# A routed mixture-of-experts layer: first token tile dense during routing, 21 steps over seven tiles, second bias on VectorE, step weights by dynamic DMA

## What is computed

```python
def reference(X, ...):                       # X [1, 1024, 256]
    Q, K, V = split(X @ W_in.T + b_in)       # rotary on the first half of Q and K
    A = sum_over_tokens(K / |K| * V)
    x = layernorm(X + (A * Q) @ W_out.T + b_out + X)
    probs = softmax(x @ gate_w)              # [1024, 8]
    score, idx = top_k(probs, 2)             # normalised to sum 1
    combine = onehot(idx) * score * alpha    # [1024, 8], two entries a row
    h = gelu(x @ fc1_w[e] + fc1_b[e])        # per expert, 256 to 256
    y = h @ fc2_w[e] + fc2_b[e]
    out = layernorm(x + sum_e combine[:, e] * y)
```

## Time and profile before

| | us |
|---|---|
| median of three runs | 142.26 |
| lowest, highest | 141.44, 142.46 |
| span of the profiled execution, first to last instruction | 139.7 |
| TensorE matmul busy in it | 117.2 (84%) |
| weight load on TensorE | 99.4 (71%) |
| VectorE, ScalarE, GpSimd busy | 71.7, 63.6, 50.9 |
| mean granted clock of TensorE | 0.936 |

### The profile page before, as it was taken

The page is one execution under the profiler, slowest core; times in us unless marked ns, Lnnn a source line. Parts: engine busy times, 40 slices in busy tenths (PEclk is TensorE's granted clock), DMA queues, the critical chain, the costliest instruction groups (busy, mean ns, idle before and its releaser), DMA issues.

```text
span 139.7 us, 2236 instructions
## 1 busy us (share of the span) xinstructions
PE 117.2 (84%) x696; PEld 99.4 (71%) x696; DVE 71.7 (51%) x209; ACT 63.6 (45%) x156; POOL 50.9 (36%) x77
## 2 busy tenths in 40 slices
PE   7799998997989838587899999999999999606920
PEld 7678887796879728475788888888888887603800
DVE  0459858796776897769433332523121222023480
ACT  3535968434653000437448475665745426000270
POOL 3008998177000001832454335574534434300000
PEclk9999999999997896899999999999999999995595
DMA  3899999951222000221122121231221221278235
GB/s 110 250 320 426 399 353 348 348 165 46 109 75 80 0 0 0 77 75 42 38 82 68 42 75 38 70 113 49 75 75 46 69 69 48 75 229 284 88 125 175
DMA packets 11209, 18.01 MB, mean 129 GB/s; under 512 B 1269, under 2 KB 7614, under 8 KB 10942
## 3 DMA queue, kind: packets, MB, share of 16 engines
q1 hardware_dynamic: 9662, 13.68, 28.8%
q0 software_dynamic: 1536, 4.20, 9.4%
HBM read 13.68 MB, written 4.19 MB: 128 GB/s over the span
## 4 chain that ended last, share of the span: by engine, by line
PE 48%; DVE 18%; POOL 11%; DMA 10%; SPq 4%; issue 4%; ACT 2%; DVEq 1%; POOLq 0%
PE ps L1148 16%; PE ps L1136 14%; PE ps L1146 5%; DMA gT_hi<-pair_rows 4%; DMA bo<-in_b_out 4%; POOL x L371 3%; POOL x L372 2%; PE ps L1119 2%; DVE lane_hot L811 2%; DMA pair_rows<-kv,scatter_i 2%; SPq L306 2%; PE ps L1040 2%; PE ps L964 2%; POOL kv L375 2%; PE ps L1029 1%
## 5 line engine op out<-in xcount | busy, mean ns | idle before, releaser
L1136 PEld LDWEIGHTS ps<-early,w_now 128*128 128x128 f32 x184 | 23.9, 191 | 3.4 <-issue 2.4
L1136 PE MATMUL ps<-early,w_now 128*128 (+1 forms) x184 | 24.5, 276 | 1.8 <-DVE early L874 1.8
L1148 PE MATMUL ps<-wres,g 128*128 x92 | 26.0, 405 | 0.0
L915 DVE SCALAR_TENSOR_TENSOR kv<-ps,w_step,kv 128x256 f32 x23 | 11.1, 483 | 28.4 <-PE ps L1148 23.7
L549 ACT ACTIVATE g<-ps,b_step 128x128 f32<-128x128 f32 x46 | 14.4, 364 | 23.6 <-PE ps L1136 23.5
L413 POOL DMA_INDIRECT pair_rows<-kv,scatter_i x16 | 15.6, 973 | 15.2 <-DVE kv L915 13.6
L972 PE MATMUL ps<-ones 128*128 128x128 f32 x100 | 17.7, 351 | 2.6 <-DVE pick_b L869 1.6
L406 POOL DMA_INDIRECT gT_hi<-x_rows,gather_i x8 | 8.4, 1048 | 28.6 <-DVE gather_i L824 20.9
L565 ACT COPY w_now<-wres 128x512 f32 x23 | 14.0, 616 | 10.4 <-issue 10.4
L972 PEld LDWEIGHTS ps<-ones 128*128 128x128 f32 x100 | 16.7, 260 | 2.8 <-issue 1.8
L1148 PEld LDWEIGHTS ps<-wres,g 128*128 128x128 f32 x92 | 15.6, 189 | 4.1
(11 more groups left out here) (181 smaller groups left out, 209.9 us busy)
## 6 DMA issues: line engine op xcount, KB each, us to landing
wres<-in_expert_w SPq DMA_DIRECT2D x8, 512.0 KB, 9.1
early<-in_x_t SPq DMA_DIRECT2D x4, 256.0 KB, 5.8
acc<-in_x_tok SPq DMA_DIRECT2D x1, 1024.0 KB, 8.6
rT<-in_rope_t SPq DMA_DIRECT2D x1, 1024.0 KB, 9.9
x_rows<-x SPq DMA_DIRECT2D x4, 256.0 KB, 2.6
gT_hi<-pair_rows SPq DMA_DIRECT2D x4, 256.0 KB, 3.7
gT_lo<-pair_rows SPq DMA_DIRECT2D x4, 256.0 KB, 6.4
out<-z SPq DMA_DIRECT2D x4, 256.0 KB, 2.2
```

Of the source, the lines that this page charges most:

```text
L915: v.scalar_tensor_tensor(out=part, in0=two(Y_BANK, s), scalar=w_step[:, s:s + 1], in1=part, op0=ALU.mult, op1=ALU.add).then_inc(y_ok, 1)
L1136: last = nc.tensor.matmul(two(H_BANK, s)[:, tile(m)], w1_now[:, s % W1_SLOTS, k, tile(m)], x[:, tile(k)], start=k == 0, stop=k == KD - 1)
L1148: last = nc.tensor.matmul(dst, g[:, s % 2, k, :], weights(KD + k, s), start=False, stop=k == KD - 1)
```

## The change

- The routed part takes tiles 1 to 7 only: 1792 choices, 14 tiles of slots, 21 steps. All tables, lists and buffers of the routing shrink accordingly.
- Tile 0 is computed dense: each of the 8 experts on its 128 tokens (`dense_fc1`, `dense_fc2`), scaled by that token's entry of `combine` (`comb0`, zero for experts not chosen) on ScalarE, added up on GpSimd (`dense_add`) onto `x1`. Its second bias is one product of `comb0T` with the 8 bias rows. Seven experts stand in TensorE's order between gates and steps, in the place of the warming products there, the eighth behind the last step. GpSimd does four of the adds before its first gather, four between the fourth and fifth gather, and one behind the last scatter.
- The alpha and tanh parts of the weights move: the weights wt are worked out before VectorE waits for the positions, alpha after the one-hot lists.
- The second bias of a step is added by VectorE, as `y_plus`, from all bias rows held on every partition (`b2_all`, a 1 MB load ahead of tables and expert weights); TensorE waits for this first instruction (`y_read`) before it writes the bank again. The bias product, `pick_b2` and the conversion of `b2` on GpSimd go.
- A step's first weights come from memory into one of four slots by an SP DMA whose source is offset by a register (`experts`, loaded on SP), 256 KB each; the copies on ScalarE and its register loads go. The slots lie in what was `rT`.
- The end: no pair for tile 0; odd tiles are added by VectorE, tiles 2, 4, 6 by GpSimd, none by TensorE, and its 12 warming products go.

```diff
-STEPS = 23
+STEPS = 21
-W1_SLOTS = 3
+W1_SLOTS = 4
...
+            sp.dma_start(b2_all[:], fc2_b.rearrange("e d -> (e d)").partition_broadcast(P)).then_inc(l_b2_all, 16)
             sp.dma_start(tab[:], tables).then_inc(l_tab, 16)
...
+            sp.wait_ge(e_no_ok, 1)
+            experts = loaded(SP, e_no, E - 1, "counts of E - 1 comparisons")
+            for s in range(STEPS):
+                if s >= W1_SLOTS:
+                    sp.wait_ge(fc1_mm, s - W1_SLOTS + 1)
+                sp.dma_start(w1_now[:, s % W1_SLOTS, :, :],
+                             expert_w[bass.ds(experts[s], 1), :, 0:KD, :].rearrange("e p k d -> p (e k) d"))\
+                  .then_inc(w1_in[s % W1_SLOTS], 16)
             sp.wait_ge(scattered, 16 * TS)
-            for t in range(T):
+            for t in range(FIRST_ROUTED, T):
...
+            def dense_add(n):
+                pool.wait_ge(d_y_ok, n + 1)
...
+            pool.wait_ge(x1_ok, 1)
+            for n in range(4):
+                dense_add(n)
...
             pool.wait_ge(idx_ok, 1)
+            for i in range(GATHERED_FIRST):
+                gather(i)
+            for n in range(4, DENSE_AHEAD + 1):
+                dense_add(n)
+            for i in range(GATHERED_FIRST, TS):
+                pool.wait_ge(xs_ok, i - GATHERED_FIRST + 2)
                 gather(i)
             pool.wait_ge(scatter_ok, 1)
             for i in range(TS):
                 scatter(i)
+            for n in range(DENSE_AHEAD + 1, E + 1):
+                dense_add(n)
+            for t in POOL_SUMS:
+                pool.wait_ge(l_pair[t], 16)
+                g_.tensor_tensor(acc[:, t, :], pair(t, 0), pair(t, 1), ALU.add).then_inc(pool_sum_ok, 1)
...
             x1_across(4)
+            a.copy(x0T[:], x1T[:, 0, :, :]).then_inc(x0T_ok, 1)
...
             a.activation(th[:], gap[:], ACT.Tanh, scale=0.5).then_inc(th_ok, 1)
+            def dense_gelu(e):
+                act.wait_ge(d_fc1_mm, e + 1)
...
+            def dense_out(n):
+                act.wait_ge(d_fc2_mm, n + 1)
+                if n >= 2:
+                    act.wait_ge(d_sum_ok, n - 1)
...
+            dense_gelu(0)
+            dense_gelu(1)
+            act.wait_ge(comb0_ok, 1)
+            dense_out(0)
+            act.wait_ge(comb0T_mm, 1)
+            a.copy(comb0T[:], ps[0:E, COMB_BANK, 0:P]).then_inc(comb0T_ok, 1)
+            for e in range(2, DENSE_AHEAD):
+                dense_gelu(e)
+                dense_out(e - 1)
+            dense_out(DENSE_AHEAD - 1)
+            dense_out(DENSE_AHEAD)
...
+                v.tensor_tensor(y_plus[:, s % 2, :], two(Y_BANK, s), b2_all[:, bass.ds(at_expert, D)],
+                                ALU.add).then_inc(y_read, 1)
+                dve.wait_ge(y_read, s + 1)
...
-                v.scalar_tensor_tensor(out=part, in0=two(Y_BANK, s), scalar=w_step[:, s:s + 1], in1=part,
+                v.scalar_tensor_tensor(out=part, in0=y_plus[:, s % 2, :], scalar=w_step[:, s:s + 1], in1=part,
...
-            stay_warm(WARM_ROUTE[0], WARM_BANK)
...
+            dense_fc1(0)
+            dense_fc1(1)
+            dense_fc2(0)
+            places()
+            dense_fc1(2)
+            pe.wait_ge(comb0_ok, 1)
+            nc.tensor.transpose(ps[0:E, COMB_BANK, 0:P], comb0[:], ident[:]).then_inc(comb0T_mm, 1)
+            dense_fc2(1)
+            dense_fc1(3)
+            dense_fc2(2)
+            inverted(0)
+            inverted(1)
+            dense_fc1(4)
+            inverted(2)
+            inverted(3).then_inc(inv_mm, 1)
+            dense_fc2(3)
+            for e in range(5, DENSE_AHEAD):
+                dense_fc1(e)
+                dense_fc2(e - 1)
+            dense_fc2(DENSE_AHEAD - 1)
+            dense_fc2(DENSE_AHEAD)
             pe.wait_ge(w_off_ok, 1)
             e_off = loaded(PE, w_off, (E - 1) * D, "counts of E - 1 comparisons")
...
-                pe.wait_ge(w1_now_ok, s + 1)
+                pe.wait_ge(w1_in[s % W1_SLOTS], 16 * (s // W1_SLOTS + 1))
...
-                nc.tensor.matmul(dst, pick_b2[:, s:s + 1].to_broadcast([BIAS_ROWS, P]), b2_parts[:], start=True, stop=False)
...
-            stay_warm(WARM_TAIL, WARM_BANK)
...
+            pe.wait_ge(g_ok, 2 * STEPS)
+            pe.wait_ge(y_read, STEPS)
+            for e in range(DENSE_AHEAD, E):
+                dense_fc1(e)
+                dense_fc2(e + 1)
```

More of the change, by code:

```diff
@@ L541, in _ @@
             a.activation(th[:], gap[:], ACT.Tanh, scale=0.5).then_inc(th_ok, 1)
+            def dense_gelu(e):
+                act.wait_ge(d_fc1_mm, e + 1)
+                if e >= 2:
+                    act.wait_ge(d_fc2_mm, e - 1 if e <= DENSE_AHEAD + 1 else e)
+                for m in range(KD):
+                    a.activation(g0[:, e % 2, m, :], two(H_BANK, e)[:, tile(m)], ACT.Gelu,
+                                 bias=b1[:, e, m:m + 1]).then_inc(d_g_ok, 1)
+            def dense_out(n):
+                act.wait_ge(d_fc2_mm, n + 1)
+                if n >= 2:
+                    act.wait_ge(d_sum_ok, n - 1)
+                e = dense_expert(n)
+                a.activation(y0[:, n % 2, :], two(Y_BANK, n), ACT.Copy,
+                             scale=1.0 if n == DENSE_AHEAD else comb0[:, e:e + 1]).then_inc(d_y_ok, 1)
             def gelu(s):
@@ L906, in _ @@
             dve.wait_ge(w_step_ok, 1)
+            dve.wait_ge(l_b2_all, 16)
             def y_add(s):
                 dve.wait_ge(fc2_mm, s + 1)
+                at_expert = nc.s_assert_within(s * D - offs[s], 0, (E - 1) * D,
+                                               skip_runtime_bounds_check_because="a step's expert is the step less its tile")
+                v.tensor_tensor(y_plus[:, s % 2, :], two(Y_BANK, s), b2_all[:, bass.ds(at_expert, D)],
+                                ALU.add).then_inc(y_read, 1)
+                dve.wait_ge(y_read, s + 1)
                 dve.wait_ge(acc0_ok, min(s + 1, TS))
@@ L1104, in _, with dense_fc1, dense_fc2 @@
-            stay_warm(WARM_ROUTE[2], WARM_BANK)
+            def dense_fc1(e):
+                if e >= 2:
+                    pe.wait_ge(d_g_ok, 2 * e - 2)
+                for m in range(KD):
+                    for k in range(KD):
+                        last = nc.tensor.matmul(two(H_BANK, e)[:, tile(m)], wres[:, k, e, tile(m)], x0T[:, k, :],
+                                                start=k == 0, stop=k == KD - 1)
+                last.then_inc(d_fc1_mm, 1)
+            def dense_fc2(n):
+                if n >= 2:
+                    pe.wait_ge(d_y_ok, n - 1)
+                if n == DENSE_AHEAD:
+                    pe.wait_ge(comb0T_ok, 1)
+                    nc.tensor.matmul(two(Y_BANK, n), comb0T[:], b2[:], start=True, stop=True).then_inc(d_fc2_mm, 1)
+                    return
+                e = dense_expert(n)
+                pe.wait_ge(d_g_ok, 2 * e + 2)
+                for k in range(KD):
+                    last = nc.tensor.matmul(two(Y_BANK, n), g0[:, e % 2, k, :], wres[:, KD + k, e, :],
+                                            start=k == 0, stop=k == KD - 1)
+                last.then_inc(d_fc2_mm, 1)
@@ new lines, in _, with places @@
+            flat = chosen[:].rearrange("p t e -> p (t e)")
+            def places():
+                pe.wait_ge(earlier_ok, 1)
+                pe.wait_ge(all_ones_ok, 2)
+                pe.wait_ge(z_ok, T)
+                pe.wait_ge(chosen_ok, 1)
+                nc.tensor.matmul(ps[:, POS_BANK, 0:(RT + 1) * E], earlier[:], flat, start=True, stop=False)
+                for back in range(1, RT + 1):
+                    last = nc.tensor.matmul(ps[:, POS_BANK, back * E:(RT + 1) * E], all_ones[:], flat[:, 0:(RT + 1 - back) * E],
+                                            start=False, stop=back == RT)
+                last.then_inc(pos_mm, 1)
@@ new lines, in inverted @@
+            def inverted(group):
+                pe.wait_ge(tile_id_ok, group + 1)
+                pe.wait_ge(hot_ok, group + 1)
+                for i in range(*HOT_GROUPS[group]):
+                    last = nc.tensor.matmul(ps[:, INV_BANK, INV_AT:INV_AT + 3 * TS], lane_hot[:, i, :],
+                                            tile_id[:, i, :, :].rearrange("p a j -> p (a j)"),
+                                            start=i == 0, stop=i == 2 * RT - 1)
+                return last
+            pe.wait_ge(l_exp, 16 * E)
@@ L1228 @@
         everywhere(np.arange(SLOT_TILES) * P),
[L1229 to L1230 removed]
+        everywhere(np.tile(tiles[T - ROUTED:], 2)),
+        everywhere(np.repeat(np.arange(2), ROUTED)),
         everywhere(np.arange(E)[None, :] < np.arange(E)[:, None]),
         lanes[:, None],
[L1233 removed]
         everywhere(np.arange(STEPS)),
```

269 lines of the change are left out of this document (126 added, 143 removed).

## The result

The median of four runs is 131.48 us (129.00 to 132.97), that of the kernel before beside them 142.36. The same kernel run again with the experiments gave 129.74 (ratio 0.913, 0.903 to 0.923). The forecast was 133.7, with 130.8 as the lower end of its wider range, and 0.914 of 142.26 is 130.0: right in direction, too small in size. The profiled execution is that of 129.00; its span is 12.8 us shorter than in the earlier trace rows.

The account below looks back on a forecast made before the run. TensorE's unbroken chain was taken to bound the loop, VectorE the stretch before it. Loop -10.0, routing +3.1, last step 0, end -1.7 sum to -8.6: 142.26 to 133.7 us; range 131.5 to 136, wider 130.8 to 138.

Parts of the forecast that it names:

- the price of the bias product: Loop: removing it saves 0.28 us per step, bounds 0.12 and 0.31; steps 1.98 us, or 2.20 with a transpose.
- a slow first step: Loop start: 0.3 us added to the loop for VectorE's register load.
- Rival (a): Loop: the bias product's pause stays with fc2, 0.11 saved per step for 0.28; +3.2, 136.9 us; chance 0.14.
- Routing: Stretch before the loop: dense experts of tile 0 make fc1(2) start 3.1 us later; bounds +1.5 and +5.
- The positions: Routing stretch: position products queue behind fc2(0), so VectorE reads them at 49.0 instead of 47.06, +1.9 us.
- its register load: Routing stretch: TensorE's load of 21 values, 2.1 us, uncovered after dense work; first transpose 59.94 to 63.5, +3.6.
- rival (b): Routing stretch: GpSimd (POOL) becomes the queue that counts, gather 4 some 3.5 us late; +3, 136.7 us; chance 0.10.
- The end: After the loop: last sum +0.5, bias products -0.6, net 0; final reload and statistics -1.7 us.
- The dense tile's last expert: After the last y sum: expert 7 of tile 0, 4.6 us, done before the first pair lands.
- the 1 MB bias load: Start: 2.9 us more loading, all in at 34 before weights are read at 43; costs nothing, otherwise up to +2.9.
- rival (c): Loop: weight loads run the four slots dry, step 2.65 us; +9.8, 143.5 us; chance 0.08 shared with all-dense-work-at-lower-clock.
- Rival (d): Routing stretch: dense experts run at lower clock; +10, 143.7 us; partly 0.05, whole within 0.08 shared with slow weight loads.

Follow-up runs that it names:

- a_evict0_late: The kernel after with VectorE's first eviction moved behind the plan's first three instructions; 129.05 us, ratio 0.910 to the kernel before.
- a_extra_load: The kernel after with one more 256 KB load at the head of the final reload, nothing computed from it; 133.66 us (one run).
- b_tail_sums: The kernel before with only the pair sums moved off TensorE to GpSimd and VectorE, eight pairs as before; 141.57 us, ratio 0.995.
- b_bias_dve: The kernel before with only the second bias moved from a TensorE product to VectorE, with its 1 MB load; 133.01 us, ratio 0.934.
- a_w1_act: The kernel after with the steps' first weights copied by ScalarE again instead of loaded by SP's DMA; 131.26 us, ratio 0.924 to the kernel before.
- a_again: The kernel after, unchanged, run again beside the experiments; 129.74 us, ratio 0.913 to the kernel before.
- b_all_again: The kernel before with every part of the change except the dense tile, second run; 136.49 us, ratio 0.956.
- a_late_behind2: The kernel after with the late first eviction and two experts of tile 0 behind the loop instead of one; 132.50 us, ratio 0.937.

## Why the prediction fell short

**The failed step is the price of the bias product.** I bounded it by 0.12 and 0.31 us and took 0.28; it was 0.51. The upper end wasn't one. It came from "fc2 to fc1 and fc1 to the bias product cost no such pause in the chain (both take 0.97 to 0.98 from start to start)". That equality showed only that both had the same pause. The eight products of an fc1 take 0.89 and the four of an fc2 0.865 when nothing with fewer rows stands next to them. The trace of before held the hint: the bias product of the earlier trace rows (99.82) and its weight load began at the same moment, and so did fc2 (100.13) and its:

```profile
99.82 0.18 PEld L1146 LDWEIGHTS ps<-b_parts,pick_b 40*128 40x128 f32 x1
100.13 0.73 PEld L1148 LDWEIGHTS ps<-wres,g 128*128 128x128 f32 x4
```

18 steps by 1.98 - 1.755 = 0.225 are 4.05 us; 0.9 went back in a slow first step and the wait at 80.51 beyond the 0.3 allowed, and 3.1 are left, the whole difference in the loop's line. Rival (a) had the sign of this doubt wrong: fc2 kept no pause, it lost one.

**Routing: right in sum (+3.3 for +3.1, where 1 us is the line's own spread), with two errors that cancel.** The positions came 1.5 us later from the mark, not 1.9. TensorE stood for its register load behind the last dense product, as forecast, but that product ended at 61.4, not 62.0, and the transpose followed 0.8 us later: most of the 1.8 us load ran beside the products. So it came at 62.20 and not 63.5, from the mark 2.8 us later and not 3.6. From there I took half a us off and half a us came on: L938 and L940 took 0.63 and 1.02 us, 0.34 and 0.59 before for slightly more columns. That is rival (b)'s mechanism at another place. They ran beside GpSimd's four adds (62.68, 3.46 us); in a_evict0_late, ahead of the adds, they took 0.33 and 0.53. There L959, beside the adds now, took 0.87 instead of 0.47. DMA traffic is not the reason: the core moved 215 GB/s beside the slow one and 242 beside the fast one. The Trainium skill (GPSIMD Engine Reference, Specifications) names contention of GpSimd with VectorE instructions that have two SBUF inputs. The trace agrees in that these instructions read two SBUF operands, while evictions from PSUM stayed at 0.42; but not each instruction with two was slowed (beside the adds of a_evict0_late L952 and L956 took 0.31 and 0.47, as elsewhere). It did not reach the loop as (b) feared: the y sums kept 0.42 and 0.48, and gather 4, issued at 66.29, was not waited for.

**The end: right mechanism, terms too small.** Tile 3 came at +5.0, not +6.5. I took 0.8 us off the fourth load's 7.3 for one load less; a_extra_load shows 1.7 us for it, and b_tail_sums 1.0 for the sums. Between last fc1 and reload, TensorE's part fell by 0.50 (-0.6 forecast) and VectorE's grew by 0.66 (+0.5); another 0.3 came on GpSimd, whose last two scatters are issued one behind the other (107.79 and 109.06). In b_bias_dve, without the rest of the change, the stretch is 7.0 us as before.

**Costs at nothing.** The dense tile's last expert was hidden, with 2.7 us to spare; the 1 MB bias load ended with the others: the queue was full until the tenth slice, 32 us, and the weights were first read after 42. The weight loads never held a step up, so rival (c) is out: a_w1_act has the same step. Rival (d) did not come true for the twelve products it priced (0.97 and 1.00 from 46 to 61.4 us). Dense work came up from the lower level and stayed at the upper there, as the rule weighed in the prediction has it (the Trainium skill, TensorE: Matmul & The Clock Gate, the HAM clock gate). In a_again it did so only later: the clock fell to half during the dense fc1 products, between 44 and 45 us, and was back between 51 and 52. That cost about 1 us, a tenth of what (d) priced. In the profile of the kernel after the clock fell again behind the dense products, where VectorE's plan covered the loss.

**The chances.** Faster by over 1% had 0.90 and came. The low end, 130.8, was too high since the bias product's bounds were not bounds. With 1.755 per step as the lower end the range would have reached 130.8 - 4.05 = 126.8, but no row of before gives that step; the runs did.

## What to carry to other kernels

Price a product that is removed by the distance between its neighbours without it, not by its own start-to-start time, and look whether the weight loads around it start together with their products: here the neighbours then paid too. Keep products in a dense sequence on the same number of rows; zeros in unused rows are cheaper than a short product (2.26 to 1.87 us per step here). When work fills a stretch that was idle, watch what it leaves behind it: a register load that had been hidden, vector work beside GpSimd's, and later positions and gathers took back 3.3 of the 16.0 us won in the loop and at the end. And count from a point behind what varies anyway: one kernel here looked 5 us slower because its first stretch was 4.5 us longer.

## What the hardware showed

- A float32r product of 256 columns on 40 or 64 rows between float32 products on 128 costs 0.39 us over its own 0.12. On 128 rows it costs 0.12.
- Gathers of a tile landed in 2.8 us (median) without the 256 KB weight loads (before, a_w1_act). With them in the loop the medians were 4.2 and 3.8 in the two profiles of the kernel after and 3.4 in b_all_again; the longest was about 6 (a_evict0_late).
- GpSimd's adds and several of VectorE's instructions with two SBUF operands slowed each other: 0.34 to 0.63, 0.59 to 1.02 and 0.47 to 0.87 us on VectorE, 0.73 to 0.87 per add on GpSimd. At the end of a_late_behind2 a pair's sum on VectorE beside such an add took 0.87 us at 369 GB/s of DMA traffic; without one, in the kernel after, it took 0.43 at 377. Instructions reading PSUM beside them kept their time.
- After two short stands of TensorE, at 61.4 and 62.6 us, the granted clock was 0.50 from 64 to 66 us although TensorE was busy all of that time. The same two stands did not always do it: in a_again (0.75 and 0.54 us) and a_evict0_late (0.77 and 0.43) the clock stayed at 1.00.
